# Attention beside an int8 linear layer on one core: the steady state's PSUM, VectorE's small work and SyncE's order rebuilt

## Chip, cores and metric

One core of a Trainium2 chip. The metric is device time in microseconds (us), the median of several runs. TensorE (PE) multiplies, VectorE (DVE), ScalarE (ACT) and GpSimd (POOL) do elementwise work, and SyncE (SP) issues every DMA of this kernel. GpSimd has no operand in PSUM here.

## The reference

For `x` of 8 sequences of 1024 tokens and 256 columns, float32:

```python
xn = layernorm(x)
q = xn @ Wq.T   # 16 heads of 16; k, v: 8 heads of 16, each used by 2 query heads
e = q k^T + alibi_bias              # -|i - j| * 2^-(head + 1)
attn = softmax(e / 4) @ v           # over all 1024 keys, no mask
a = attn @ Wo.T + bo
scale = max(|xn|) / 127             # per token
f = (round(xn / scale) as int8 @ weight_q.T) * scale * weight_scale + bias
out = x + a + f
```

## The kernel before

**Units and tiles.** There are 64 tiles of 128 tokens and 64 units; unit u is one sequence with one key head and its two query heads. A unit computes scores twice. The *row* scores (queries on partitions, `ps_row`) give each query's maximum over all keys; the *column* scores (keys on partitions) are computed with that maximum as two further contraction rows, so that exp can be applied straight away and its result multiplied with the values. q and k are split into three bfloat16 parts (`parts`), written to DRAM, and loaded back per unit as a *row set* (10 DMAs) and a *column set* (10 DMAs and then, for each of two heads, 2 small DMAs of maxima, `place_max`). Alongside, every unit prepares one later tile (11 ahead: normalise, quantise, project to q, k, v, the int8 product) and finishes one earlier tile (9 behind: the output projection).

**Order.** Each engine runs its own written-out order; semaphores join them. `SEGMENTS` cuts the 64 units into stretches with the same set of jobs. In one unit TensorE does 16 steps (s): each computes one 128x1024 block of column scores (`col_block`, two halves of 512) and one block of row scores two units ahead (`row_block`). Every second step it does a value product (`pv_block`, float32). Products whose result has 128 rows are issued as four matmuls of 32 weight columns each (`in_strips`); the tile preparation and projections use whole 128-column weights (L825, L833, L836, L850, L950).

**PSUM.** 8 banks: two row blocks of two banks (`ps_row`), two banks of column scores (`ps_col`), one for values (`ps_pv`), and one, `ps_work`, for everything else. A row block waits until VectorE has reduced the block two before (L635, `reduce_block`). A column half waits until ScalarE's exp (L797) of the same half one step before is done. Seven jobs a unit share `ps_work`, in this order: `turn_max` 0 (L899), `project`, `turn_xn`, `turn_max` 1, `make_qkv`, `turn_xq`, `make_lin`.

**VectorE** reduces 16 row blocks a unit, two after each even step. Between them stand, in this order: `turn_pv` (L660), `find_stats` (L548), `split_max`, `finish` (output sum), `normalise` and `find_scale` (L558 to L571), `quantise`, `find_rest`, `norm` (L667, L674, L681: divides by the softmax sum, gives `att_unit` of the unit before), `split_max`, `scale_lin`.

**GpSimd** multiplies the diagonal blocks of the exp results by the bias on them (L520, `weigh_near`, 8 a unit), and does `find_rstd`, `gather_v`, `find_low` (L481) and `add_linear` (L488, L490).

**SyncE** in one unit: load x, load `att_t` (L359), the column set of unit u+1 (L319, L326), `place_max` 0 (L340), `store_out` (L440), `place_max` 1, the row set of unit u+3, `store_parts` (L297), `store_att` of unit u-1 (L351, two DMAs, waits for `att_unit_ready`). TensorE begins a unit only when all 14 DMAs of its column set have landed:

```python
pe.wait_ge(col_set_loaded[par], 16 * COL_SET * ((u - par) // 2 + 1))
```

## Time and profile before

| | |
|---|---|
| runs | median 1769.76 us of 3 (1768.62 to 1770.13) |
| the profiled execution | 1769.02 us, span 1767.2 us |
| granted TensorE clock, mean | 0.988 |
| TensorE busy | 1707.5 us, 97% |
| VectorE busy | 1594.3 us, 90% |
| ScalarE busy | 1243.0 us, 70% |
| GpSimd busy | 591.9 us, 33% |

A busy TensorE is not TensorE at its peak, as matmuls overlap and their ends are modelled. A "PEld" is a weight load, which runs beside a matmul. "Idle before" names what ended an engine's idle time. DMA issues are SyncE's queue ("SPq"). A row of the timeline has its start and how long it took, in us, and how many instructions it merges.

### The profile page before, as it was taken

What the parts mean: (1) busy time and instruction counts of PE and PEld (TensorE: products, weight loads), DVE (VectorE), ACT (ScalarE), POOL (GpSimd) and SP (SyncE); (2) the same over time, 40 slices, a digit from 0 to 9 for tenths busy, and PEclk for the clock granted to TensorE, in tenths of its full rate; (3) what the DMA queues carried; (4) which work ended last, traced back from release to release, by engine and by line L of the source; (5) the groups of instructions that cost most, each with busy time, mean ns of one, the idle gap of its engine ahead of it and who ended that gap; (6) DMA issues with size and microseconds to landing.
All of it is one profiled execution on the core that took longest, in us unless ns stands there. A gap on an engine that the chain in (4) does not pass through costs nothing.

```text
span 1767.2 us, 68604 instructions
## 1 busy us (share of the span) xinstructions
PE 1707.5 (97%) x22272; PEld 719.4 (41%) x22272; DVE 1594.3 (90%) x2306; ACT 1243.0 (70%) x2498; POOL 591.9 (33%) x904
## 2 busy tenths in 40 slices
PE   6799999999999999999999999999999999999997
PEld 4234443443443443443443443443444444333333
DVE  6899999999999999999999999999999999999991
ACT  3267777777777777777777777777777777777775
POOL 4323333333333333333333333333333333222221
PEclk9799999999999999999999999999999999999999
DMA  4322223223223223223223223223233222222222
GB/s 117 86 71 76 65 70 80 71 79 86 75 78 85 76 78 85 75 79 85 75 79 84 74 81 84 74 81 83 75 81 84 74 81 80 71 72 68 72 63 70
DMA packets 184331, 137.99 MB, mean 78 GB/s; under 512 B 102649, under 2 KB 143865, under 8 KB 184281
## 3 DMA queue, kind: packets, MB, share of 16 engines
q1 hardware_dynamic: 184280, 137.34, 28.8%
q8 instruction: 29, 0.48, 0.1%
q14 instruction: 22, 0.17, 0.0%
HBM read 101.06 MB, written 35.65 MB: 77 GB/s over the span
## 4 chain that ended last, share of the span: by engine, by line
PE 69%; DVE 19%; issue 7%; DMA 1%; DVEq 1%; ACT 1%; SPq 1%; POOL 0%; POOLq 0%; ACTq 0%
PE ps_row L884 20%; PE ps_col L884 19%; PE ps_pv L943 18%; DVE row_max L635 13%; PE ps_work L833 5%; PE ps_work L950 3%; DVE att_normed L674 2%; DVE rest L591 2%; PE ps_work L836 1%; PE ps_work L825 1%; PE ps_work L850 1%; ACT probs L797 1%; DVE rsum L667 1%; DMA bias<-bias_lin 0%; DVEq L231 0%
## 5 line engine op out<-in xcount | busy, mean ns | idle before, releaser
L797 ACT ACTIVATE probs<-ps_col 128x512 f32<-128x512 f32 x2024 | 1098.4, 595 | 293.4 <-PE ps_col L884 293.0
L635 DVE TENSOR_REDUCE row_max<-ps_row 128x1 f32<-128x1024 f32 x1024 | 1201.2, 1213 | 64.4 <-PE ps_row L884 62.8
L520 POOL TENSOR_TENSOR probs<-probs,near 128x256 f32<-128x256 f32 x512 | 376.8, 736 | 1074.0 <-ACT probs L797 1074.0
L884 PE MATMUL ps_col<-q_col,k_col 122*32 122x512 bf16 x8096 | 657.0, 383 | 0.5 <-ACT probs L797 0.4
L884 PE MATMUL ps_row<-k_row,q_row 120*32 120x512 bf16 x8192 | 579.0, 386 | 23.2 <-DVE row_max L635 18.2
L943 PE MATMUL ps_pv<-probs,v_unit 128*32 128x512 f32 x4096 | 530.9, 594 | 3.1 <-POOL probs L520 2.9
L884 PEld LDWEIGHTS ps_col<-q_col,k_col 122*32 122x32 bf16 x8096 | 202.7, 94 | 548.3 <-ACT probs L797 428.6
L884 PEld LDWEIGHTS ps_row<-k_row,q_row 120*32 120x32 bf16 x8192 | 193.5, 95 | 212.7 <-DVE row_max L635 139.6
L943 PEld LDWEIGHTS ps_pv<-probs,v_unit 128*32 128x32 f32 x4096 | 119.6, 110 | 82.4 <-issue 11.9
L833 PE MATMUL ps_work<-xn_t,wqk 128*128 128x128 f32 x636 | 85.1, 284 | 0.0
L833 PEld LDWEIGHTS ps_work<-xn_t,wqk 128*128 128x128 f32 x636 | 75.0, 191 | 22.5 <-issue 22.5
L744 ACT ACTIVATE v_all<-ps_work 128x128 f32 (+1 forms) x53 | 14.7, 277 | 89.8 <-PE ps_work L836 89.8
L660 DVE STREAM_TRANSPOSE pv_turned<-ps_pv 128x512 f32<-128x512 f32 x64 | 45.2, 706 | 20.4 <-PE ps_pv L943 20.4
L950 PE MATMUL ps_work<-wo,att_t 128*128 128x256 f32 x224 | 63.3, 405 | 0.0
L781 ACT ACTIVATE neg_max_t<-ps_work 16x128 bf16<-16x128 bf16 x128 | 34.0, 266 | 37.4 <-PE ps_work L899 34.3
L481 POOL TENSOR_TENSOR parts<-rest,parts 128x384 bf16<-128x384 f32 x64 | 59.1, 923 | 0.9 <-ACT parts L753 0.7
L490 POOL TENSOR_TENSOR base<-base,lin 128x256 f32 (+1 forms) x64 | 46.8, 731 | 11.6 <-POOL base L488 11.2
L488 POOL TENSOR_TENSOR base<-base,bias 128x256 f32 (+1 forms) x64 | 47.1, 736 | 9.7 <-DVE lin L598 8.0
L950 PEld LDWEIGHTS ps_work<-wo,att_t 128*128 128x128 f32 x224 | 37.9, 189 | 27.1 <-issue 24.2
L689 DVE TENSOR_TENSOR out_tile<-ps_work,base 128x256 f32<-128x256 f32 x55 | 23.4, 425 | 20.9 <-issue 15.9
L739 ACT ACTIVATE xn_t<-ps_work 128x256 f32<-128x256 f32 x53 | 20.3, 383 | 29.8 <-PE ps_work L825 29.8
L475 POOL TENSOR_TENSOR rstd<-rstd,half_pow 128x1 f32<-128x1 f32 x64 | 35.8, 559 | 11.9 <-POOL rstd L472 11.0
(74 smaller groups left out, 807.4 us busy)
## 6 DMA issues: line engine op xcount, KB each, us to landing
parts_dram<-parts SPq DMA_DIRECT2D x64, 288.0 KB, 3.2
q_row<-parts_dram SPq DMA_DIRECT2D x128, 96.0 KB
q_col<-parts_dram SPq DMA_DIRECT2D x128, 96.0 KB
q_row<-parts_dram SPq DMA_DIRECT2D x128, 64.0 KB
q_col<-parts_dram SPq DMA_DIRECT2D x128, 64.0 KB
att_dram<-att_unit SPq DMA_DIRECT2D x128, 64.0 KB
att_t<-att_dram SPq DMA_DIRECT2D x56, 128.0 KB, 2.2
out<-out_tile SPq DMA_DIRECT2D x55, 128.0 KB, 1.8
```

The source lines that it names most:

```text
L475: pool.tensor_tensor(rstd[:, par, 1:2], rstd[:, par, 0:1], half_pow[:, :], ALU.pow).then_inc(rstd_ready, 1)
L481: pool.tensor_tensor(parts[:, par, 2, :], rest[:, par, :], parts[:, par, 1, :], ALU.subtract).then_inc(low_ready, 1)
L488: pool.tensor_tensor(here, here, bias[:, :], ALU.add).then_inc(base_ready, 1)
L490: pool.tensor_tensor(here, here, lin[:, par, :], ALU.add).then_inc(base_ready, 1)
L520: pool.tensor_tensor(here, here, near[:, bass.ds(u % KV_HEADS, 1), :].rearrange("p a (e n) -> p (a e) n", e=GROUP), ALU.mult).then_inc(wei ...
L635: dve.tensor_reduce(row_max[:, e, qb:qb + 1], ps_row[qb % 2][:, :], AX_X, ALU.max).then_inc(row_max_found, 1)
L660: dve.transpose(pv_turned[:, :], ps_pv[:, :]).then_inc(pv_read, 1)
L797: act.activation(probs[:, c % PBUFS, e, h * HALF:(h + 1) * HALF], col_bank(f, s, h), ACT.Exp, scale=SCALE).then_inc(exp_done, 1)
L833: pe.matmul(bank[:, m * P:(m + 1) * P], wqk[:, c, m * P:(m + 1) * P], xn_t[:, c, :], start=(c == 0), stop=(c == EC - 1))
L884: mm = pe.matmul(to[at, :], weights[:, at], moving, start=start, stop=stop)
L943: mm = pe.matmul(ps_pv[32 * j:32 * j + 32, :], v_unit[:, par, c, :], probs[:, c % PBUFS, j // 2, (j % 2) * HALF:(j % 2 + 1) * HALF], start ...
L950: mm = pe.matmul(bank, att_of_tile[:, c, :], wo[:, c, :], start=(c == 0), stop=(c == EC - 1))
```

## The change

- **PSUM.** `ps_col` and `ps_work` become a ring of three banks, `ps_ring`. 36 items a unit go through it in a fixed order: the 32 column halves, and after blocks 2, 5, 6 and 7 one item each: `early_max` (the maxima of head 0), `turns` (`xn` and `xq` turned, the maxima of head 1), `qkv`, `outputs` (the int8 product and the output projection). TensorE fills an item's bank when the item three before it has been freed; ScalarE alone reads and frees them.
- **TensorE.** Whole-width products of the steady state are issued in four strips; `turn_xn` becomes a float32 product with the identity. The value product of block c moves from step 2c + 3 to block c + 2's steps.
- **VectorE** keeps the reductions, `find_stats`, `turn_pv`, `normalise`, `find_scale` and `norm`, after blocks 0, 1, 2, 2 and 3. `norm` thus stands after reduction 8 of 16, where it stood after 12.
- **GpSimd** takes `split_max` (the reduction now negates), `quantise`, `split_qk` (all four steps of the splitting of q and k), `weigh_linear` and `finish`.
- **ScalarE** copies q and k unsplit, scales the int8 product per token, copies the projection.
- **SyncE's order** becomes: x (12 ahead, was 11), `att_t`, column set u+1, `store_parts` of the tile before, `place_max` 0, `store_att` of unit u-1, row set u+3, `store_out`, `place_max` 1.

The diff, cut to its core:

```diff
@@ module level and PSUM
+    others = {2: "early_max", 5: "turns", 6: "qkv", 7: "outputs"}
+    for c in range(BLOCKS):
+        items += [(c, e, h) for e in range(GROUP) for h in range(2)]
+        if c in others:
+            items.append(others[c])
-        ps_col = [ctx.enter_context(nc.psum_tensor(f"ps_col{i}", [P, HALF], F32)) for i in range(2)]
+        ps_ring = [ctx.enter_context(nc.psum_tensor(f"ps_ring{i}", [P, HALF], F32))
+                   for i in range(BANKS)]
-        ps_work = ctx.enter_context(nc.psum_tensor("ps_work", [P, HALF], F32))
@@ sync: unit
-                if f["prep"]:
-                    if f["proj"]:
-                        wait_apart(sp, out_ready, u - OUT_BEHIND)
-                    next_x(u + PREP_AHEAD)
+                if f["next_x"]:
+                    next_x(u + X_AHEAD)
                 if f["proj"]:
                     load_att_t(u - OUT_BEHIND, (par + OUT_BEHIND) % 2)
...
-                    wait_apart(sp, col_scores, 2 * SLOTS * u)
+                    wait_apart(sp, ring_filled, ITEMS * u)
                     load_col_set(u + 1, 1 - par)
+                if f["lag"]:
+                    store_parts(u + PREP_AHEAD - 1, (par + PREP_AHEAD - 1) % 2)
+                if not f["last"]:
                     place_max(u + 1, 1 - par, 0)
-                if f["proj"]:
-                    store_out(u - OUT_BEHIND, (par + OUT_BEHIND) % 2)
-                if not_last:
-                    place_max(u + 1, 1 - par, 1)
+                if f["prev"]:
+                    store_att(u - 1)
                 if f["row_set"]:
...
                     load_row_set(u + 3, 1 - par)
-                if f["prep"]:
-                    store_parts(u + PREP_AHEAD, (par + PREP_AHEAD) % 2)
-                if f["prev"]:
-                    store_att(u - 1)
+                if f["out"]:
+                    store_out(u - OUT_BEHIND - 1, (par + OUT_BEHIND + 1) % 2)
+                if not f["last"]:
+                    place_max(u + 1, 1 - par, 1)
@@ gpsimd
+            def split_qk(t, par):
+                wait_apart(pool, ring_freed, ITEMS * (t - PREP_AHEAD) + PLACE["qkv"] + 1)
+                wait_apart(pool, parts_stored[par], 16 * ((t - par) // 2))
+                pool.tensor_copy(parts[:, par, 0, :], qk[:, par, :]).then_inc(high_ready, 1)
...
+                pool.tensor_tensor(rest[:, par, :], qk[:, par, :], parts[:, par, 0, :],
+                                   ALU.subtract).then_inc(rest_ready, 1)
...
+                pool.tensor_copy(parts[:, par, 1, :], rest[:, par, :]).then_inc(middle_ready, 1)
+                find_low(t, par)
...
+                if f["prev"] and not f["last"]:
+                    split_max(GROUP * u + 2, 0)
+                if f["lag"]:
+                    split_qk(t - 1, 1 - tpar)
                 for c in range(BLOCKS):
                     weigh_near(u, c)
+                    if c == 0 and f["prep"]:
+                        find_rstd(t, tpar)
+                    if c == 1 and f["lag"]:
+                        weigh_linear(t - 1, 1 - tpar)
+                        add_linear(t - 1, 1 - tpar)
...
                     if c == 2 and f["prep"]:
+                        quantise(t, tpar)
+                    if c == 3 and f["row_heads"] >= 1:
+                        split_max(GROUP * u + 3, 1)
+                    if c == 3 and f["out"]:
+                        finish(u - OUT_BEHIND - 1, (par + OUT_BEHIND + 1) % 2)
@@ vector: unit
+                for c in range(BLOCKS):
+                    for i in (2 * c, 2 * c + 1):
+                        if i < BLOCKS and f["row_heads"] >= 1:
+                            reduce_block(GROUP * u + 3, 1, i)
+                        if i >= BLOCKS and f["row_heads"] >= 2:
+                            reduce_block(GROUP * u + 4, 0, i - BLOCKS)
+                    if c == 0 and f["prep"]:
...
+                        find_stats(t, tpar)
+                    if c == 1 and f["prev"]:
                         turn_pv(u - 1)
+                    if c == 2 and f["prep"]:
                         normalise(t, tpar)
                         find_scale(t, tpar)
-                    if s == 11 and f["prev"]:
+                    if c == 3 and f["prev"]:
                         norm(u - 1)
@@ tensor
+            def take_bank(u, item):
+                if not (isinstance(u, int) and ITEMS * u + PLACE[item] < BANKS):
+                    pe.wait_ge(ring_freed, ITEMS * u + PLACE[item] - BANKS + 1)
+                return ring_bank(item)
...
+                for c in range(BLOCKS):
+                    if c == 0:
+                        pe.wait_ge(col_set_loaded[par], 16 * COL_SET * ((u - par) // 2 + 1))
+                    col_half(u, par, c, 0, 0)
+                    col_half(u, par, c, 0, 1)
+                    ahead_row_block(u, par, f, 2 * c)
+                    col_half(u, par, c, 1, 0)
+                    if c >= 2:
+                        pv_block(u, par, c - 2)
+                    elif f["prev"]:
+                        pv_block(u - 1, 1 - par, BLOCKS - 2 + c)
+                    col_half(u, par, c, 1, 1)
+                    ahead_row_block(u, par, f, 2 * c + 1)
...
```

## Rows read from the trace of the kernel before

**Rows 1.** The page: busy time of each engine (share of the span), and the chain that ended last

```profile
PE 1707.5 (97%) x22272; PEld 719.4 (41%) x22272; DVE 1594.3 (90%) x2306; ACT 1243.0 (70%) x2498; POOL 591.9 (33%) x904
...
PE 69%; DVE 19%; issue 7%; DMA 1%; DVEq 1%; ACT 1%; SPq 1%; POOL 0%; POOLq 0%; ACTq 0%
...
L739 ACT ACTIVATE xn_t<-ps_work 128x256 f32<-128x256 f32 x53 | 20.3, 383 | 29.8 <-PE ps_work L825 29.8
```

**Rows 2.** The transpose in `turn_pv`, once a unit, in three stretches: ns min/median/max, first and last start

```profile
L660 DVE STREAM_TRANSPOSE pv_turned<-ps_pv x9: 703/704/707, 122.0 to 329.4; 128x512 f32<-128x512 f32 x9
...
L660 DVE STREAM_TRANSPOSE pv_turned<-ps_pv x44: 704/706/707, 356.0 to 1496.9; 128x512 f32<-128x512 f32 x44
...
L660 DVE STREAM_TRANSPOSE pv_turned<-ps_pv x8: 704/705/707, 1520.6 to 1687.9; 128x512 f32<-128x512 f32 x8
```

**Rows 3.** The chain that ended last, in order of time: start us, us, what

```profile
802.24 0.55 PE ps_col L884 x8
802.79 0.86 PE ps_pv L943 x8
...
805.03 0.43 PE ps_col L884 x8
...
813.31 1.06 PE ps_work L950 x4
...
819.89 1.53 PE ps_work L833 x12
```

**Rows 4.** Timeline of VectorE in one unit, with the TensorE row ahead of one reduction

```profile
807.02 0.70 DVE L660 STREAM_TRANSPOSE pv_turned<-ps_pv 128x512 f32<-128x512 f32 x1
...
812.43 0.42 DVE L548 BATCH_NORM_STATS2 stats<-base 128x6 f32 x1
...
813.11 2.35 DVE L635 TENSOR_REDUCE row_max<-ps_row 128x1 f32<-128x1024 f32 x2
...
816.60 0.41 DVE L558 TENSOR_SCALAR xn<-base,mean_var,rstd 128x256 f32 x1
...
817.86 2.35 DVE L635 TENSOR_REDUCE row_max<-ps_row 128x1 f32<-128x1024 f32 x2
...
821.80 0.61 PE L884 MATMUL ps_row<-k_row,q_row 120*32 120x512 bf16 x8
...
822.47 1.22 DVE L635 TENSOR_REDUCE row_max<-ps_row 128x1 f32<-128x1024 f32 x1 [0.21 <-PE ps_row L884]
...
824.08 0.24 DVE L667 RECIPROCAL rsum<-pv_turned 128x16 f32<-128x16 f32 x1
...
825.10 0.45 DVE L681 STREAM_TRANSPOSE att_unit<-att_normed 128x256 f32<-128x256 f32 x1
```

**Rows 5.** Timeline of SyncE's queue (DMA issues) in one unit

```profile
815.86 1.52 SPq L340 DMA_DIRECT2D q_col<-neg_max_t  x2
817.74 0.40 SPq L440 DMA_DIRECT2D out<-out_tile  x1
819.41 1.36 SPq L340 DMA_DIRECT2D q_col<-neg_max_t  x2
821.65 1.74 SPq L319 DMA_DIRECT2D k_row<-parts_dram  x3
...
828.21 0.31 SPq L326 DMA_DIRECT2D k_row<-k_alibi  x1
...
830.01 1.58 SPq L351 DMA_DIRECT2D att_dram<-att_unit  x2
```

**Rows 6.** Timeline where TensorE waits for the first row set

```profile
61.69 0.40 SPq L326 DMA_DIRECT2D k_row<-k_alibi  x1
...
63.60 1.90 PE L884 MATMUL ps_row<-k_row,q_row 120*32 120x512 bf16 x16 [3.69 <-DMA k_row<-k_alibi]
```

**Rows 7.** Timeline of GpSimd in one unit

```profile
801.11 0.92 POOL L481 TENSOR_TENSOR parts<-rest,parts 128x384 bf16<-128x384 f32 x1
...
805.59 0.73 POOL L490 TENSOR_TENSOR base<-base,lin 128x256 f32 x1 [0.19 <-POOL base L488]
```

More of the change, by code:

```diff
@@ L711, in unit @@
                         normalise(t, tpar)
                         find_scale(t, tpar)
-                    if s == 9 and f["prep"]:
-                        quantise(t, tpar)
-                    if s == 11 and f["prep"]:
-                        find_rest(t, tpar, work[1])
-                    if s == 11 and f["prev"]:
+                    if c == 3 and f["prev"]:
                         norm(u - 1)
-                    if s == 14 and f["row_heads"] >= 2:
-                        split_max(GROUP * u + 4, 0)
@@ L721, in unit @@
-                    if s == 15 and f["prep"]:
-                        scale_lin(t, tpar, work[0])
             run_units(dve, unit)
@@ L800, in unit @@
[L800 to L815 removed]
+                keep_first_max(e)
@@ new lines, in unit @@
+            def unit(u, par, f):
+                for item in RING_ITEMS:
+                    if item == "early_max":
+                        if f["last"]:
+                            keep_nothing(u, item)
+                        else:
+                            wait_item(u, item)
+                            keep_max_t(u, par, 0, ring_bank(item))
+                    elif item == "turns":
+                        if f["last"]:
+                            keep_nothing(u, item)
+                        else:
+                            keep_turns(u, par, f)
+                    elif item == "qkv":
+                        if f["prep"]:
+                            keep_qkv_whole(u, par)
+                        else:
+                            keep_nothing(u, item)
+                    elif item == "outputs":
+                        keep_outputs(u, par, f)
+                    else:
+                        exps(u, *item)
@@ L946, in pv_block, with ahead_row_block, turn_nothing @@
                 mm.then_inc(pv_done, 1)
+            def ahead_row_block(u, par, f, i):
+                if i < BLOCKS and f["row_heads"] >= 1:
+                    row_block(GROUP * u + 3, 1 - par, 1, i)
+                if i >= BLOCKS and f["row_heads"] >= 2:
+                    if i == BLOCKS:
+                        wait_row_set(u + 2, par)
+                    row_block(GROUP * u + 4, par, 0, i - BLOCKS)
+            def turn_nothing(u, item):
+                bank = take_bank(u, item)
+                pe.transpose(max_turn(bank), eye_b[:, 0:MAX_ROWS * BLOCKS], eye_b[:, :]).then_inc(
+                    ring_filled, 1)
@@ new lines, in outputs @@
+            def outputs(u, par, f):
+                t, bank = u + PREP_AHEAD, take_bank(u, "outputs")
+                if f["prep"]:
+                    pe.wait_ge(xq_t_ready, t + 1)
+                    for c in range(EC):
+                        mm = in_strips(bank[:, 0:EMBED], xq_t[:, c, :], w8[:, c, :], c == 0,
+                                       c == EC - 1)
+                if f["proj"]:
+                    pe.wait_ge(att_t_loaded, 16 * (u - OUT_BEHIND + 1))
+                    opar = (par + OUT_BEHIND) % 2
+                    for c in range(EC):
+                        mm = in_strips(bank[:, EMBED:2 * EMBED], att_t[:, opar, c, :], wo[:, c, :],
+                                       c == 0, c == EC - 1)
+                else:
+                    mm = pe.transpose(max_turn(bank), eye_b[:, 0:MAX_ROWS * BLOCKS], eye_b[:, :])
+                mm.then_inc(ring_filled, 1)
@@ L948, in project @@
+            run_units(pe, unit)
+            for c in (BLOCKS - 2, BLOCKS - 1):
+                pv_block(UNITS - 1, (UNITS - 1) % 2, c)
             def project(att_of_tile, bank):
```

386 lines of the change are left out of this document (212 added, 174 removed).

## The prediction, made before the run

> **What bounds the kernel now.** I read the page's shares first: TensorE 97% busy, VectorE 90%, ScalarE 70%, GpSimd 33%, and the chain that ended last is 69% TensorE and 19% VectorE [rows 1]. Then the period, from the transpose that runs once a unit [rows 2]: (329.4 - 122.0) / 8 = 25.9 us while no projection runs, (1496.9 - 356.0) / 43 = 26.5 us over the long middle, (1687.9 - 1520.6) / 7 = 23.9 us when no tile is left to prepare. So time is a period times a number of units, and the change has to be costed as a period.
>
> What of the 26.5 us is TensorE streaming? In the chain [rows 3] eight strip matmuls of 512 columns take 0.43 us. At 2.4 GHz one such stream is 0.213 us, so four strips run together. A value product takes 0.86 us. Per unit: 32 blocks (16 column, 16 row) x 0.43 = 13.8; 8 x 0.86 = 6.9; q, k, v: 8 float32 products of 128 columns, each a quarter of the 0.86, 1.7; projection 2 x 0.43 = 0.86; the rest about 0.5. Sum 23.8. The other 2.7 us are waits and changes between whole weights and strips: the column block behind the whole-width product takes 0.55 against 0.43, and the projection 1.06 against 0.86 [rows 3]; that is 0.12 on the way out and perhaps as much or a little more on the way in, so for five such places a unit I estimate 1.0 to 1.3 us. VectorE's busy 1594.3 us are 24.9 us a unit [rows 1], so it is close behind TensorE. These two bound the kernel together; SyncE and GpSimd don't.
>
> **TensorE's part.** Strips remove the changes (-1.0 to -1.3 us). The ring removes the wait for the exp of the step before (the remainder, some 0.6 us). `turn_xn` as a float32 product streams twice as long, +0.2. New streaming: about 24.3 us, if strips of 128 columns run four abreast as those of 512 do. The trace has no such strip. Lower bound: they stream as above. Upper bound: they cost by the matmul, at the nearest row 0.43 / 8 = 54 ns each [rows 3]; 112 small strip matmuls (64 + 16 + 16 + 8 + 8) would take 6.0 us where they stream 3.3, +2.7 us. I take the lower bound, since 54 ns is what the stream itself accounts for, and keep the upper as a rival. The Trainium skill (TensorE: Matmul & The Clock Gate, Back-to-back issue gap) gives about 81 ns a matmul for sustained weight-load and matmul pairs at 128 columns; by it the 112 small matmuls would take 9.1 us, and the sum of TensorE's own chain would be 5.8 us longer. The row's 54 ns is already under that figure, so the rule doesn't fit this strip form, though no run here shows the narrow ones.
>
> **VectorE's part.** It loses `split_max`, `quantise`, `find_rest`, `finish`, `scale_lin`, some 3 us of 24.9, so about 21.7 us are left: it has slack on average. But what stays is bunched after blocks 0 to 3, in front of the first eight reductions. I lay one unit out from its first column matmul (time 0). A row block can be reduced 0.67 us after its first matmul starts (821.80 to 822.47) and a reduction takes 1.17 (2.35 / 2) [rows 4]. Row 0 starts at 0.43, row 1 at 2.17. Reduction 0 runs from 1.10 to 2.27, reduction 1 from 2.84 to 4.0; `find_stats` 0.68 (812.43 to 813.11) to 4.7; two reductions to 7.0; `turn_pv` 0.70 to 7.7; two reductions to 10.1; `normalise` and `find_scale` 1.26 (816.60 to 817.86) to 11.3; two reductions to 13.7; `norm` 1.47 (824.08 to 825.55), so `att_unit` is ready at **15.1** [rows 4].
>
> TensorE feels this. Row 8 waits for reduction 6 (12.5) where it would be due at 10.9, row 10 for reduction 8 (16.2) where it would be due at 13.5. The stall adds up to 2.7 us and isn't given back, since blocks 5 to 7 carry TensorE's extra products. Add about 0.6 us where the ring waits for ScalarE: the item `turns` takes three evictions (0.38 each for the larger two [rows 1]) before the third next half may use its bank. TensorE's own chain: 24.3 + 2.7 + 0.6 = **27.6 us**, already over 26.5. The gains of the first part are real and are spent here.
>
> **SyncE's part, which I expect to end last.** A unit starts only when `place_max` 1 has landed. Before, that was issued at 819.41, ahead of the row set; then came row set, `store_parts`, `store_att`, with nothing waiting soon. After, `store_att` of unit u-1, which waits for the `norm` above, stands ahead of the row set, and `place_max` 1 behind it. Everything behind the waiting `store_att` is late. From `att_unit` ready [rows 5]: wait and address work 0.36 (as 817.38 to 817.74); `store_att` 1.58; three waits and address work 0.88 (820.77 to 821.65); the row set's ten issues, 821.65 to 828.52, 6.87; 0.36 and `store_out` 0.40; about 0.15 to 0.36 and 0.70 until the second small DMA is issued; then 1.91 from the issue of a last DMA to the first matmul that waits for it (61.69 to 63.60) [rows 6]. Sum 13.2 to 13.4. I take 13.2. The period is 15.1 + 13.2 = **28.3 us**, a closed loop: unit start, eight reductions, `norm`, 13 issues, unit start. Its cover before was half a unit of order; now there is none. The other reordered DMAs (x, `att_t`, the column set, `store_parts`, `place_max` 0) are out by about 11 us, before `att_unit` is ready, and hide.
>
> **GpSimd and ScalarE.** GpSimd takes 3 + 3 + 1 + 1 operations of 256 to 384 columns, each at most 0.73 to 0.92 us, with 0.19 us between dependent ones [rows 7], and 4 tiny ones: at most 10 us more on 9.2 (591.9 / 64) [rows 1], so 19 of 28 us. It could hold up `weigh_near` 0 (due at block 2) behind `split_qk`, about 5.3 us against 6.6. I cost it at nothing; without that cover each microsecond it is late is one on TensorE. ScalarE: 19.4 us (1243.0 / 64) plus less than 1.
>
> **The sum.** Units 1 to 8 have no `store_out`: 28.3 - 0.76 = 27.5 against 25.9, 8 x 1.6 = 13 us. 44 units at 28.3 against 26.5: 44 x 1.8 = 78 us. The eight units that load row sets but prepare no tile lack `find_stats` and `normalise`: `att_unit` at 13.5, period 26.7 against 23.9, 8 x 2.8 = 22 us. First unit and the larger first load of x: 2. Together +115 on the profiled execution's own 1769.0: 1884 us; the median of runs is 0.7 above that execution, so **1885 us**.
>
> **Rivals.**
> 1. *TensorE and VectorE set the period, SyncE doesn't.* If issues or landing are 0.7 us or more quicker than summed, the period is 27.6 and less early and late: 44 x 1.1 + 8 x 1.1 (27.0) + nothing late = about +57, 1826 us. For it: the two chains are close. Against: each SyncE term is a row.
> 2. *Strips cost by the matmul.* TensorE's chain is 27.6 + 2.7 = 30.3: 52 x 3.8 + 22 = about +220, 1990 us. For it: 128-column strips are nowhere in the trace.
> 3. *The other side: faster.* The loop over SyncE doesn't close, because row-set issues get shorter when they start without a full ring of column-set descriptors in flight (k_row alone took 1.74 for three [rows 5]), and GpSimd's relief lets TensorE stream. It decides only if 3.8 us go from the SyncE part and the bunching costs TensorE nothing; then 24.3 us a unit: 44 x -2.2, 8 x -2.4, 8 x -1.9 is about -131, 1638 us. It begins to be faster when 1.8 us go from SyncE's part and 1.1 from TensorE's. Against it: the issues look like SyncE's own work, the same pair of small DMAs taking 1.52 right behind the column set and 1.36 two microseconds later [rows 5].
> 4. *The change doesn't remove stalls, it moves them, and ends even*: the period is 26.5 after all, 1770 us.
>
> **Chances.** SyncE's loop, 0.55; rival 1, 0.2; rival 2 or GpSimd late, 0.11; rival 3, 0.1; rival 4, 0.04. Forecast 1885 us. Its own range is 1850 to 1920 (a landing or address gap off by 0.5 us is 26 us over 52 units). The range that leaves 2 in 10 out takes in rival 1 and half of the GpSimd cases: 1805 to 1940. About 0.2% is what a measurement of this kernel can tell from no change. Faster 0.1, same 0.04, slower 0.86.
>
> **What would show it.** In the trace after: a period of 28.3 us between `turn_pv` transposes, 26.7 late; SyncE waiting some 4 us before each `store_att`, and no other long wait; TensorE's wait at each unit's start, put down to the small DMAs of the maxima; VectorE's reductions 0 to 8 back to back, and idle after reduction 11; row-block waits of 2 to 3 us a unit behind reductions 6 and 8; no loss at the changes of weight width. In the late units TensorE would idle over 3 us at a time; should its granted clock fall there, the late period is longer than my 26.7. Wrong if `place_max` 1 is found issued well before the unit's end, if `att_unit` is ready much before 15 us, or if the small strips are far from 3.3 us a unit.

## The result, and the profile after

The changed kernel takes a median of 2021.33 us in 4 runs (2019.78 to 2029.5), against 1769.76 before (4 runs too): a ratio of 1.143 (1.140 to 1.146), 251.6 us slower. The direction was forecast, the size was not: 1885 us with a range up to 1940.

First the page: busy shares, the instruction queue among the DMA queues, and the chain that ended last, by engine and by line. Its answers before are [rows 1].

```profile
PE 1709.5 (85%) x26876; PEld 769.7 (38%) x26876; DVE 1444.4 (72%) x1736; ACT 1275.8 (63%) x2575; POOL 978.6 (49%) x1580
...
q8 instruction: 252, 4.13, 0.9%
...
PE 28%; SPq 25%; issue 20%; DVE 17%; DMA 6%; DVEq 1%; ACT 1%; POOL 0%; ACTq 0%; POOLq 0%
SPq L351 16%; PE ps_pv L1056 10%; PE ps_ring L1003 10%; PE ps_row L1003 8%; DVE row_max L730 8%; DMA q_col<-neg_max_t 5%; SPq L387 4%; SPq L376 2%; DVE att_normed L767 1%; DVE amax L660 1%; DVE xn L653 1%; DVE pv_turned L753 1%; DVE att_unit L774 1%; DVE stats L643 1%; SPq L474 1%
```

TensorE's busy time is what it was (1709.5 against 1707.5 us), but its share of the chain fell from 69% to 28%. SyncE's queue went from 1% to 25%, with nine of the row set's ten issues (L351) as the largest line of all, and "issue" (time in which an engine waited for nothing that the profile shows) from 7% to 20%. The trace of before counts 29 packets of instructions on q8 and this one 252. The prediction had no term for those. Here is the line of before:

```profile
q8 instruction: 29, 0.48, 0.1%
```

Then the period: the `turn_pv` transpose in three stretches, to be read against [rows 2].

```profile
L753 DVE STREAM_TRANSPOSE pv_turned<-ps_pv x9: 704/706/707, 123.7 to 370.9; 128x512 f32<-128x512 f32 x9
...
L753 DVE STREAM_TRANSPOSE pv_turned<-ps_pv x41: 704/706/707, 428.0 to 1664.9; 128x512 f32<-128x512 f32 x41
...
L753 DVE STREAM_TRANSPOSE pv_turned<-ps_pv x7: 705/706/706, 1748.8 to 1915.7; 128x512 f32<-128x512 f32 x7
```

That is 247.2 / 8 = 30.9 us early (forecast 27.5), 1236.9 / 40 = 30.9 in the middle (28.3) and 166.9 / 6 = 27.8 late (26.7). In the middle the units alternate between about 29.4 and 32.3 us, two to a turn of the loop.

Now the loop that was forecast to set the period, in the unit that starts at 1039.77. First VectorE's timeline, then SyncE's queue, then the end of the chain that ended last (start, us, what).

```profile
1040.97 1.22 DVE L730 TENSOR_REDUCE row_max<-ps_row 128x1 f32<-128x1024 f32 x1 [2.65 <-PE ps_row L1003]
...
1046.69 0.71 DVE L753 STREAM_TRANSPOSE pv_turned<-ps_pv 128x512 f32<-128x512 f32 x1
...
1054.68 0.45 DVE L774 STREAM_TRANSPOSE att_unit<-att_normed 128x256 f32<-128x256 f32 x1
```

```profile
1055.58 1.54 SPq L387 DMA_DIRECT2D att_dram<-att_unit  x2
1057.89 2.17 SPq L351 DMA_DIRECT2D k_row<-parts_dram  x3
1060.45 4.62 SPq L351 DMA_DIRECT2D q_row<-parts_dram  x6
1065.25 0.31 SPq L358 DMA_DIRECT2D k_row<-k_alibi  x1
1065.82 0.40 SPq L474 DMA_DIRECT2D out<-out_tile  x1
1066.42 1.50 SPq L376 DMA_DIRECT2D q_col<-neg_max_t  x2
```

```profile
1066.42 0.77 SPq L376
...
1067.24 1.77 DMA q_col<-neg_max_t
1069.01 1.45 issue
1070.46 0.62 PE ps_ring L1003 x5
```

`att_unit` is done at 1055.13, 15.4 us after the unit's start (forecast 15.1); the fifteen issues shown follow with gaps of at most 0.8 us, and the last small DMA lands at 1069.01, 13.9 us later. The next unit could begin there. It begins at 1070.46: 1.45 us go to something on no engine, "issue". SyncE's waits show the same loop over the whole run, as does TensorE's wait at a unit's start (waiter, releaser: us in total, times, longest):

```profile
SPq L274 <- DVE att_unit L774: 214.6, 56, 4.1
```

```profile
PE ps_ring L1003 <- DMA q_col<-neg_max_t: 76.2, 38, 3.3
```

56 waits of 3.8 us before `store_att` (forecast: some 4). Two things beside the loop were not forecast. The first is in TensorE's timeline and in the windows of the same stretch (from:to, us, busy and count of each engine, granted clock, DMA share, GB/s):

```profile
1008.45 0.62 PE L1003 MATMUL ps_ring<-q_col,k_col 122*32 122x512 bf16 x8 [3.01 <-issue]
...
1009.60 1.94 PE L1056 MATMUL ps_pv<-probs,v_unit 128*32 128x512 f32 x8
...
1017.91 1.06 PE L1056 MATMUL ps_pv<-probs,v_unit 128*32 128x512 f32 x8 [1.10 <-DVE pv_turned L753]
...
1026.70 0.62 PE L1003 MATMUL ps_row<-k_row,q_row 120*32 120x512 bf16 x8 [0.66 <-DVE row_max L730]
```

```profile
1008.00:1013.50 5.50, 5.05 (x56) 2.09 (x60) 1.86 (x2) 2.49 (x5) 2.20 (x4) 0.69 0.31 91
1013.50:1031.50 18.00, 15.80 (x246) 6.32 (x238) 16.25 (x22) 12.85 (x27) 11.04 (x18) 1.00 0.22 56
```

TensorE has idled 3.01 us before this unit, the last 1.72 of them after the small DMA had landed (at 1006.73, by the chain). The granted clock of the next 5.5 us is 0.69, so most of them ran at 1.2 GHz; the value product takes 1.94 us against 1.06 eight microseconds on. This unit's `att_unit` is ready 17.1 us after its start, not 15.4. The second: the value product of block 0 waits 1.10 us for `turn_pv`, which reads the same bank of values.

### The profile page after: what moved, and what is told of

Read it like the earlier page. It is cut to its first block, busy times and chain, and to the rows that moved or that the text cites. A ratio compares the mean times of both kernels' runs of the same rounds, so it can differ in the third digit from the quotient of the medians.

```text
span 2017.7 us, 77945 instructions
## 1 busy us (share of the span) xinstructions
PE 1709.5 (85%) x26876; PEld 769.7 (38%) x26876; DVE 1444.4 (72%) x1736; ACT 1275.8 (63%) x2575; POOL 978.6 (49%) x1580
## 4 chain that ended last, share of the span: by engine, by line
PE 28%; SPq 25%; issue 20%; DVE 17%; DMA 6%; DVEq 1%; ACT 1%; POOL 0%; ACTq 0%; POOLq 0%
SPq L351 16%; PE ps_pv L1056 10%; PE ps_ring L1003 10%; PE ps_row L1003 8%; DVE row_max L730 8%; DMA q_col<-neg_max_t 5%; SPq L387 4%; SPq L376 2%; DVE att_normed L767 1%; DVE amax L660 1%; DVE xn L653 1%; DVE pv_turned L753 1%; DVE att_unit L774 1%; DVE stats L643 1%; SPq L474 1%
## 5 line engine op out<-in xcount | busy, mean ns | idle before, releaser
L865 ACT ACTIVATE probs<-ps_ring 128x512 f32<-128x512 f32 x2048 | 1132.1, 595 | 493.4 <-PE ps_ring L1003 461.6
L1003 PE MATMUL ps_ring<-q_col,k_col 122*32 122x512 bf16 x8192 | 754.4, 389 | 135.4 <-DMA q_col<-neg_max_t 76.2
L1003 PE MATMUL ps_row<-k_row,q_row 120*32 120x512 bf16 x8192 | 654.1, 392 | 78.4 <-DVE row_max L730 63.5
L1003 PEld LDWEIGHTS ps_ring<-q_col,k_col 122*32 122x32 bf16 x8192 | 232.2, 97 | 525.4 <-issue 182.6
L1003 PEld LDWEIGHTS ps_row<-k_row,q_row 120*32 120x32 bf16 x8192 | 217.0, 98 | 455.8 <-DVE row_max L730 187.8
L570 POOL TENSOR_SCALAR xclip<-xn,xinv 128x256 f32<-128x256 f32 x53 | 61.1, 1152 | 73.8 <-DVE xinv L666 73.8
L1003 PE MATMUL ps_ring<-xn_t,wqk 128*32 128x128 f32 x2544 | 78.6, 272 | 0.0
L1003 PEld LDWEIGHTS ps_ring<-xn_t,wqk 128*32 128x32 f32 x2544 | 70.4, 109 | 11.1
L573 POOL TENSOR_SCALAR xround<-xclip 128x256 f32<-128x256 f32 x53 | 57.3, 1080 | 9.7 <-POOL xclip L570 9.5
L1003 PE MATMUL ps_ring<-wo,att_t 128*32 128x256 f32 x880 | 56.9, 378 | 0.0
L577 POOL TENSOR_SCALAR xq<-xround 128x256 bf16<-128x256 f32 x53 | 46.1, 871 | 14.5 <-POOL xround L573 14.3
L586 POOL TENSOR_TENSOR rest<-qk,parts 128x384 f32<-128x384 f32 x53 | 48.5, 916 | 9.5 <-POOL parts L584 9.2
```

The source lines that it names most:

```text
L570: pool.tensor_scalar(xclip[:, :], xn[:, par, :], xinv[:, par, :], Q_MAX, ALU.mult, ALU.min).then_inc(xq_ready, 1)
L573: pool.tensor_scalar(xround[:, :], xclip[:, :], -Q_MAX - 1, ROUND, ALU.max, ALU.add).then_inc(xq_ready, 1)
L586: pool.tensor_tensor(rest[:, par, :], qk[:, par, :], parts[:, par, 0, :], ALU.subtract).then_inc(rest_ready, 1)
L865: act.activation(probs[:, c % PBUFS, e, h * HALF:(h + 1) * HALF], ring_bank((c, e, h)), ACT.Exp, scale=SCALE).then_inc(ring_freed, 1)
L1003: mm = pe.matmul(to[at, :], weights[:, at], moving, start=start, stop=stop)
```

## The experiments

"On after" and "on before" say from which kernel each starts. The ratio is to the kernel before, run beside it on the same chip.

### The order of SyncE's queue

**e1_order**, on after: `store_att` last.

```diff
                     place_max(u + 1, 1 - par, 0)
-                if f["prev"]:
-                    store_att(u - 1)
                 if f["row_set"]:
...
                     place_max(u + 1, 1 - par, 1)
+                if f["prev"]:
+                    store_att(u - 1)
```

> The changed kernel with SyncE's order alone altered: row set, store_out, place_max 1, and only then store_att. Theory A (the period is a loop over SyncE: unit start, norm, store_att, row set, place_max 1, unit start; 29.4 us in the undisturbed units, 31.0 us on average): the loop is gone, TensorE's own chain with VectorE is left, about 28 us a unit, and the time falls to 1840 to 1880 us. Theory B (what costs is the reload of TensorE's instructions in each loop turn, with the half clock behind it): the reload stays, the time stays within 20 us of 2020. Theory C (TensorE's and VectorE's bunched work is the period anyway): less than 60 us are gained.

Measured: 1940.99 us, 1.098 (1.094 to 1.101), 80 us faster than after. Its chain has 1% of SyncE's queue where after has 25%:

```profile
PE 53%; DVE 20%; issue 18%; ACT 3%; POOL 2%; DVEq 2%; DMA 1%; SPq 1%; ACTq 1%; POOLq 0%
```

The loop is gone, and the kernel is still 171 us slower than before. Its units in the middle alternate between 28.2 us and 30.5 to 32.6, and it still counts 252 packets on q8. None of the three theories had this size: more than the 60 us of theory C, less than theory A's. The hole at the unit's start is there without SyncE's loop too:

```profile
921.18 0.61 PE L1003 MATMUL ps_ring<-q_col,k_col 122*32 122x512 bf16 x8 [2.95 <-issue]
```

So something besides the loop costs more than the loop does.

**e5_before_order**, on before: the other way round, `store_att` put ahead of the row set and `place_max` 1 behind it, where `norm` stands after reduction 12.

```diff
-                if not_last:
-                    place_max(u + 1, 1 - par, 1)
+                if f["prev"]:
+                    store_att(u - 1)
                 if f["row_set"]:
...
-                if f["prev"]:
-                    store_att(u - 1)
+                if not_last:
+                    place_max(u + 1, 1 - par, 1)
```

> The kernel before with one edit, SyncE's order: store_att ahead of the row set, and place_max 1 last in the unit. Nothing else is changed, and its turn of the loop fits. Theory A (a loop over SyncE): att_unit is ready 22.1 us after the unit's first matmul (803.48 to 825.55), and 13 to 14 us of issues and landing follow, so 35 to 37 us a unit: 2250 to 2400 us. Rival (SyncE's order matters little, since its queue has 10% to spare): 1769 to 1800 us.

Measured: 2429.59 us, 1.373 (1.370 to 1.376), slower than expected; the page's chain has SPq 22%, SPq L319 15% of it. The middle's 41 periods are 37.6 us each:

```profile
L660 DVE STREAM_TRANSPOSE pv_turned<-ps_pv x42: 716/717/718, 422.2 to 1963.0; 128x512 f32<-128x512 f32 x42
```

TensorE waits so long at each unit's start that its mean granted clock is 0.865 in this run, against 0.988 before. With a later `norm` the same order costs 11 us a unit (37.6 against 26.5): the loop is shown from both sides.

### Strips or whole weights

**e2_wide**, on after: the tile's products on whole 128-column weights again (and `xn` turned by a transpose, as before), all else as after.

```diff
-                        in_strips(bank[:, m * P:(m + 1) * P], wqk[:, c, m * P:(m + 1) * P],
-                                  xn_t[:, c, :], c == 0, c == EC - 1)
+                        pe.matmul(bank[:, m * P:(m + 1) * P], wqk[:, c, m * P:(m + 1) * P],
+                                  xn_t[:, c, :], start=(c == 0), stop=(c == EC - 1))
...
```

> The changed kernel with the five products of the tile work on whole 128-column weights again, so that TensorE has some 336 instructions fewer in a turn of the loop. Theory A plus B: the instruction transfers inside the loops vanish as in the kernel before (29 in all, not 252), the granted clock stays at 1.00 in the long stretch, and every second unit no longer takes 3 us more: period 29.4 us in all units, time 1930 to 1950 us. Theory A alone: the period is SyncE's loop and does not move, 2015 to 2025 us. If the changes of weight width were worth more than all that, the time would be above 2021.

Measured: 1922.66 us, 1.087 (1.083 to 1.091), 99 us faster than after. The edit brings back the changes of width, whose removal was forecast as a gain of 1.0 to 1.3 us a unit. Here are the transpose and the q8 packets of the same stretch, first of e2, then the packets of after from 428 to 1665 us:

```profile
L753 DVE STREAM_TRANSPOSE pv_turned<-ps_pv x42: 705/706/707, 435.0 to 1616.7; 128x512 f32<-128x512 f32 x42
```

```profile
q8 instruction: 4, 0.07, 0.0%
```

```profile
q8 instruction: 180, 2.95, 1.0%
```

28.8 us a unit, nearly the same from unit to unit (28.6 to 29.0 us), and 4 packets in the stretch where after has 180 (nine to a turn of the loop, 16 KB each). This is the forecast loop alone: 28.8 where 28.3 was summed. The time is a little under the 1930 to 1950 us that were expected. But the chain of e2 has as large a share of "issue" as that of after:

```profile
SPq 26%; PE 26%; issue 20%; DVE 19%; DMA 6%; DVEq 1%; ACT 1%; POOL 0%; POOLq 0%; ACTq 0%
```

So that share doesn't measure the loading of instructions.

**e3_order_wide**, on after: the diffs of e1 and e2 together.

> Both edits: SyncE's order and whole 128-column weights. Theory A plus B: no loop over SyncE and no reload. What is left is TensorE's chain with VectorE's bunched work, 27.6 us by the forecast's sum plus 1.0 to 1.2 for the width changes, minus what was already counted twice: 27.5 to 28.5 us a unit, 1820 to 1870 us. If the bunching does not cost what the forecast said, the period is 25 to 26.5 us and the time 1690 to 1770 us.

Measured: 1869.46 us, 1.057 (1.054 to 1.060). So the order is worth 53 us where no instructions are loaded (e2 to e3) and 80 where they are (after to e1); strips cost 72 us without the loop (e3 to e1) and 99 with it. The period of e3 is 1050.9 / 37 = 28.4 us (431.4 to 1482.3 us, 38 transposes): the chain of TensorE and VectorE, forecast at 27.6 with strips.

**e4_before_strips**, on before: the five products in strips, order and PSUM as before.

```diff
-                        make_qkv(t, work[1])
+                        strips_qkv(t, work[1])
...
-                        project(att_t[:, (par + OUT_BEHIND) % 2, :, :], work[1][:, 0:EMBED])
+                        strips_project(att_t[:, (par + OUT_BEHIND) % 2, :, :],
+                                       work[1][:, 0:EMBED])
...
-                        turn_xn(t, tpar, work[0])
+                        strips_xn(t, tpar, work[0])
...
```

> The kernel before with the one edit that its five whole-width products of the steady state are issued in strips. Theory B (the longer instruction stream of a loop turn is loaded anew each turn, and TensorE waits for it): some 9 instruction transfers in each turn, 1.5 to 4 us lost in each of 26 turns, half clock after some of them, against at most 1 us a unit gained from the width changes: 1770 to 1850 us. Rival (a reload hides, only the width changes count): 1.0 us a unit faster, about 1710 us. Rival 2 of the prediction (strips cost by the matmul): 2.7 us a unit slower, about 1910 us.

Measured: 1947.81 us, 1.102 (1.098 to 1.105): 178 us slower by this edit alone, far over the 1770 to 1850 us that theory B gave. TensorE's timeline across the end of a loop's turn, the windows around it and the q8 packets from 930 to 960 us:

```profile
939.32 1.03 PE L943 MATMUL ps_pv<-probs,v_unit 128*32 128x512 f32 x8
942.95 0.39 PE L884 MATMUL ps_col<-q_col,k_col 122*32 122x512 bf16 x2 [2.60 <-issue]
946.08 1.04 PE L884 MATMUL ps_col<-q_col,k_col 122*32 122x512 bf16 x6 [2.74 <-issue]
946.49 2.34 PE L884 MATMUL ps_row<-k_row,q_row 120*32 120x512 bf16 x16
```

```profile
918.00:935.00 17.00, 16.99 (x301) 8.07 (x305) 16.21 (x26) 11.87 (x25) 4.83 (x9) 1.00 0.24 71
935.00:952.00 17.00, 11.33 (x147) 4.71 (x137) 9.59 (x12) 7.01 (x15) 4.57 (x7) 0.80 0.33 91
952.00:970.00 18.00, 17.63 (x319) 8.40 (x313) 16.78 (x27) 12.42 (x26) 4.67 (x8) 1.00 0.13 37
```

```profile
q8 instruction: 6, 0.10, 1.3%
```

Nobody is waited for at 939 to 946 us: two column matmuls are issued between two holes of 2.6 and 2.7 us. The packets are spread over the 30 us, and one comes in during each hole (the same view counts one from 939.5 to 942.9 and one from 943.4 to 946.0). That the packets of q8 are TensorE's is inferred: only TensorE's program grew in e4, and q8 goes from 29 packets to 269 over the run while the other instruction queue, q14, stays at 21 (22 before). Then the clock is down (0.80 over the window) and sixteen matmuls take 2.34 us that take 1.04 elsewhere. A unit without this takes 27.0 us, one with it 33.9: about 7 us a turn. The 27.0 is itself over before's 26.5, so the undisturbed unit doesn't gain by the strips either.

**e8_before_unroll4**, on before: `UNROLL = 4` for 2, so that each turn of the loop holds four units. No product changes, and each unit does what it did.

```diff
-UNROLL = 2
+UNROLL = 4
```

> The kernel before, untouched but for UNROLL 4 instead of 2: the same instructions in the same order, a turn of the loop twice as long (about 3046 records of TensorE in four units, not 1523 in two). Theory B (a turn that does not fit TensorE's instruction store is loaded anew and TensorE waits at its start): instruction transfers in every turn, about 7 us lost in each of 13 turns, with the half clock after them: 1840 to 1880 us. Rival (the strips themselves cost what e4_before_strips lost): 1765 to 1772 us.

Measured: 1845.57 us, 1.044 (1.041 to 1.047), as expected. From 360 to 1484 us it has 130 packets on q8 (and 161 on a second instruction queue, q14) where before has 3; the four units of a turn take 26.5, 31 to 32.4, 27.3 and 26.5 us. The strips' streaming is out of the question here: the size of the loop's body brings the packets, and the loss comes with them. The body grows for every engine in e8, so it is e4 that ties the loss to TensorE's.

**Where it begins.** Three more on before put fewer products into strips: **e9_before_qkv_strips** q, k and v alone (the first two lines of e4's diff), **e13_before_small_strips** the others without those, **e14_before_most_strips** all but the int8 product and the turn of `xq`.

> The kernel before with only the q, k, v product in strips: 192 records more in a turn, about 1715 of TensorE. It looks where the store ends. Theory B, store smaller than 1715: transfers in each turn, 6 to 7 us lost per turn, 1930 to 1950 us. Store larger: 29 transfers in all, no loss, and 0.0 to 0.3 us a unit less for one width change, 1755 to 1770 us.

> Where TensorE's instruction store ends: the kernel before with all but q, k, v in strips, 152 records more in a turn, 1675. In e9_before_qkv_strips 1715 fitted in the middle (26.26 us a unit), but units 1 to 8 loaded. If the store holds a number of instructions between 1715 and 1867: no transfers in the middle, 26.0 to 26.4 us a unit there. Units 1 to 8 (no projection, fewer records) show whether it is the number alone: with it, they fit too.

> The kernel before with q, k, v, the projection and the turning of xn in strips: 296 records more in a turn, 1819. Either it fits (26.0 to 26.5 us a unit, about 1765 us) and the store ends between 1819 and 1867, or it loads in each turn as e4_before_strips does (27 and 34 us, about 1945 us) and ends between 1715 and 1819. If the loss grew with the number of instructions over the store and not by the turn, it would be clearly less than the 7 us a turn of e4_before_strips.

Measured: 1769.99 us, 1.0007 (0.9991 to 1.0024); 1911.62 us, 1.081 (1.078 to 1.083); 1874.88 us, 1.060 (1.057 to 1.062). e13 came out against its expectation: it loads in the middle, with fewer records than e9. e14 fell between its two cases: it loads in every turn, but a turn loses about 3 us (units of 27.0 and 30.0), not 7. So the loss doesn't grow evenly with the body. e13 holds both cases in one run. Its transposes and q8 packets, early (122 to 332 us), then in the middle (417 to 1588 us):

```profile
L660 DVE STREAM_TRANSPOSE pv_turned<-ps_pv x9: 698/699/705, 123.1 to 331.7; 128x512 f32<-128x512 f32 x9
```

```profile
q8 instruction: 7, 0.11, 0.2%
```

```profile
L660 DVE STREAM_TRANSPOSE pv_turned<-ps_pv x40: 698/709/718, 417.7 to 1588.3; 128x512 f32<-128x512 f32 x40
```

```profile
q8 instruction: 176, 2.88, 1.0%
```

Early, where the body has no projection, 26.1 us a unit (25.9 before) and hardly a packet; in the middle 30.0 and nine packets a turn. I counted TensorE's records of every kind in one turn of each loop. At 1523 (before), 1527 (e2, e3) and 1609 (e13 early) no instructions are loaded; at 1675 (e13), 1697 (e9 early), 1819 (e14), 1867 (e4), 1870 (after) and 3040 (e8) they are in every turn. But at 1715 (e9, middle) they are not, and in e12 below, at 1719, they are in every second turn. So the size decides only roughly; what decides between 1675 and 1719 wasn't settled. e9 shows what the strips of q, k and v save where nothing is loaded: 26.53 - 26.26 = 0.27 us a unit (its middle against before's), given back in the early units (27.8 us against 25.9).

### What is left: VectorE's bunch and GpSimd

**e10_before_pool**, on before: quantising and `split_max` on GpSimd, nothing else.

```diff
@@ gpsimd: unit
+                    if c == 2 and f["row_heads"] >= 1:
+                        split_max(GROUP * u + 3, 1)
+                    if c == 4 and f["prep"]:
+                        quantise(t, tpar)
...
@@ vector: unit
-                    if s == 9 and f["prep"]:
-                        quantise(t, tpar)
...
```

> The kernel before with one part of the change alone: quantise and split_max go from VectorE to GpSimd (1.7 of VectorE's 24.9 us a unit), order and PSUM as before. If VectorE's load is half of what bounds the kernel: 0.3 to 0.8 us a unit less, 1735 to 1755 us. If TensorE's streaming and width changes bound it: 1765 to 1772 us. If GpSimd's slower operations (1.15, 1.08 and 0.87 us where VectorE takes 0.34, 0.29 and 0.29) come late for turn_xq or hold up the diagonal blocks: above 1772 us.

Measured: 1768.40 us, 0.9993 (0.9983 to 1.0002): no difference, though VectorE's busy time falls from 1594.3 to 1500.0 us. This relief of VectorE alone buys nothing in the old order.

From e3 on, each of four kernels adds one edit to the one before it.

**e6_norm_late**: `norm` after block 6 for 3, out of the bunch.

```diff
-                    if c == 3 and f["prev"]:
+                    if c == 6 and f["prev"]:
                         norm(u - 1)
```

> The kernel of e3_order_wide (28.4 us a unit) with norm moved on VectorE from behind reduction 8 to behind reduction 14, where TensorE's extra products leave VectorE idle. Theory C (the bunched VectorE work stalls TensorE by the row banks, and what is bunched ahead is never given back): 1.0 to 1.4 us a unit less, 27.0 to 27.4 us, 1800 to 1815 us. Rival (TensorE has that stall anyway, from its own extra products and the ring): within 0.3 us a unit of 28.4, above 1850 us.

Measured: 1833.17 us, 1.037 (1.034 to 1.040), 36 us faster than e3, less than expected; the period goes from 28.4 to 27.8.

**e7_proj_early**: the output projection moved from the item after block 7 to the one after block 2, `finish` after block 1, and `turn_pv` directly behind the third reduction, so that the first value product need not wait for it. ScalarE gets one more small copy a unit, which frees the old item.

```diff
                     if c == 2:
...
+                        if f["proj"]:
+                            pe.wait_ge(att_t_loaded, 16 * (u - OUT_BEHIND + 1))
...
+                                mm = pe.matmul(bank[:, 0:EMBED], att_t[:, opar, k, :],
+                                               wo[:, k, :], start=(k == 0), stop=(k == EC - 1))
...
+                        if i == 2 and f["prev"]:
+                            turn_pv(u - 1)
...
-                    if c == 3 and f["out"]:
+                    if c == 1 and f["out"]:
                         finish(u - OUT_BEHIND - 1, (par + OUT_BEHIND + 1) % 2)
```

> As e6_norm_late, and the output projection moved from the item after block 7 into the item of the maxima after block 2, so that TensorE has its own extra work where VectorE is behind; turn_pv stands directly behind reduction 3 of 16, finish after block 1. Theory C: 1.0 to 1.3 us less than e6_norm_late, 25.8 to 26.3 us a unit, 1735 to 1770 us. Rival: no less than e6_norm_late.

Measured: 1807.46 us, 1.022 (1.019 to 1.025), 26 us faster, less than expected. A new wait took the rest (waits view):

```profile
ACT proj L914 <- POOL out_tile L605: 114.3, 43, 2.9
```

ScalarE waits 2.7 us a unit for `finish` on GpSimd to free the buffer of the projection, and the bank of the ring with it.

**e7b_finish_early**: `finish` behind the first diagonal block.

```diff
+                    if c == 0 and f["out"]:
+                        finish(u - OUT_BEHIND - 1, (par + OUT_BEHIND + 1) % 2)
                     if c == 0 and f["prep"]:
...
-                    if c == 1 and f["out"]:
-                        finish(u - OUT_BEHIND - 1, (par + OUT_BEHIND + 1) % 2)
```

> As e7_proj_early, and GpSimd's finish moved from behind the linear sums to directly behind the first diagonal block. In e7_proj_early ScalarE's copy of the projection waited for it, 114 us in 43 units, and with it the ring and TensorE, about 1.4 us a unit. If that wait was the last thing in TensorE's way there: 1.0 to 1.4 us a unit less than 27.4, 26.0 to 26.4 us, 1745 to 1765 us. If another wait takes its place: above 1790 us.

Measured: 1775.91 us, 1.003 (1.001 to 1.005), 32 us faster than e7 and between the two cases that were expected. The wait is gone, and GpSimd is late elsewhere:

```profile
PEld ps_pv L1060 <- POOL probs L555: 53.0, 51, 1.5
```

The value product waits for `weigh_near`, which stands behind the other work of GpSimd.

**e11_pool_order**: quantising after block 3 for 2, the sum of the int8 product after block 5 for 1.

```diff
-                    if c == 1 and f["lag"]:
+                    if c == 5 and f["lag"]:
                         weigh_linear(t - 1, 1 - tpar)
...
-                    if c == 2 and f["prep"]:
+                    if c == 3 and f["prep"]:
                         quantise(t, tpar)
```

> As e7b_finish_early, with GpSimd's order altered: quantise behind the fourth diagonal block instead of the third, the linear sums behind the sixth instead of the second. In e7b_finish_early TensorE waited about 1.5 us a unit for GpSimd at one value product (80 us in all). If that wait was the last thing in its way: 0.8 to 1.3 us a unit less than 26.7, 25.4 to 25.9 us, 1705 to 1740 us, faster than the kernel before. If the row banks or the ring take its place: 1760 to 1775 us.

Measured: **1736.11 us, 0.981 (0.980 to 0.983)**, within the time expected and faster than both kernels. Its middle:

```profile
L753 DVE STREAM_TRANSPOSE pv_turned<-ps_pv x44: 704/705/707, 379.9 to 1490.1; 128x512 f32<-128x512 f32 x44
```

25.8 us a unit against 26.5. It keeps the ring and the work moved to GpSimd and ScalarE, with the places that e6 to e11 gave the work; whole weights and `store_att` last are before's.

**e12_pool_order_strips**: e11 with q, k and v in strips.

```diff
-                        pe.matmul(bank[:, m * P:(m + 1) * P], wqk[:, c, m * P:(m + 1) * P],
-                                  xn_t[:, c, :], start=(c == 0), stop=(c == EC - 1))
+                        in_strips(bank[:, m * P:(m + 1) * P], wqk[:, c, m * P:(m + 1) * P],
+                                  xn_t[:, c, :], c == 0, c == EC - 1)
...
```

> As e11_pool_order, with q, k, v alone in strips (192 records of TensorE more in a turn). If TensorE sets the period there: 0.2 to 0.3 us a unit less in the middle, as e9_before_qkv_strips showed (26.53 to 26.26), 8 to 14 us, minus what is lost if a turn in units 1 to 8 or in the middle does not fit: a loss of 7 us a turn would show as 252 instead of 40 instruction transfers and 1850 us or more.

Measured: 1811.55 us, 1.023 (1.021 to 1.025), 75 us slower than e11, for 96 more matmuls a turn and their weight loads: its units take 25.9 us, and 31 to 32 in every second turn, where q8 has most of its packets. The 8 to 14 us that were expected as a gain are lost in it.

## Why the prediction was right in direction and wrong in size

What the loop over SyncE would do was right. The step that failed is "Strips remove the changes (-1.0 to -1.3 us)" with what follows it, "I take the lower bound": the strips were costed by their streaming alone. What a strip is besides, four instructions for one, had no term, though by the diff the tile's products go from 26 matmuls a unit to 112, and its rivals priced a stream, not a program.

Of the 251.6 us, the trace gives by stretch (after less before, from the first and last transposes): early 8 periods 247.2 - 207.4 = 40 us (forecast 13); then 43 periods from 370.9 to 1696.4 us, 1325.5 - 43 x 26.53 = 185 (forecast 78); the last nine, to 1940.4 us, 26 (forecast 22). The miss of 136 us is in the early and middle units.

- **The missing term.** after to e2 measures it, net of what the strips save: 99 us, of which none was forecast. It is time lost to holes while instructions come in and the lower clock behind them. e8 shows it with no strip added, e4 with no new order.
- **SyncE's loop**: confirmed in place and nearly in size. `att_unit` at 15.4 against 15.1 (the sum is right, though it speaks of 13 issues where there are 15); from there to the landing 13.9 and, in the unit before, 14.1 against 13.2. q_row's six issues and k_row's three took 6.8 us alone, the whole row set 7.7 against 6.87. Sum 29.3; e2 measured 28.8 against 28.3. Over 44 units that is some 22 us of the miss, and early and late units the rest. Early, e2 has 224.8 / 8 = 28.1, 0.7 under its middle, as the 0.76 for the missing `store_out` had it:

```profile
L753 DVE STREAM_TRANSPOSE pv_turned<-ps_pv x9: 704/706/707, 123.5 to 348.3; 128x512 f32<-128x512 f32 x9
```

  Late, the forecast was 1 us short in after: in the unit that starts at 1799.35 `att_unit` is ready at 14.5, where 13.5 was summed, and SyncE's part takes 13.1. The clock, which the prediction feared for there, held: 0.99 granted from 1748 to 1916 us. In e2 seven late transposes lie 28.1 us apart (1672.2 to 1841.0 us), at 0.96; why it is longer there wasn't followed.
- **TensorE's and VectorE's chain**: 27.6 forecast; e3 has 28.4 with whole weights and e1's undisturbed units 28.2 with strips. It was sized 0.6 short. The prediction's own sum shows a gap of that size: 26.5 less at most 1.3 for the changes and 0.6 for the ring, plus 0.2, is 24.8, not 24.3. Rival 1 could not have come true: even without SyncE's loop the kernel is at 1941 us.
- **Width changes** were over-sized. In after the strips of q, k, v take 1001.34 - 999.59 = 1.75 us, from their first start to the next column block's. In e3 the whole products took 1.98 (901.29 to 903.27). That is 0.23 us, and e9 gave 0.27, which is the forecast's price for one place. But the other places don't give it: e13 has three of them (all but the projection) in strips early, with hardly a packet, and takes 26.1 against 25.9, and e3 against e1 shows 0.2 for all five.
- **Rival 2 is refuted.** The same 64 matmuls in 1.75 us are 27 ns each, half of the 54 ns it priced:

```profile
999.59 1.48 PE L1003 MATMUL ps_ring<-xn_t,wqk 128*32 128x128 f32 x48
1000.90 0.61 PE L1003 MATMUL ps_ring<-wv,xn_t 128*32 128x128 f32 x16
1001.34 0.61 PE L1003 MATMUL ps_ring<-q_col,k_col 122*32 122x512 bf16 x8
```

  The narrow strips run four abreast as the wide ones do. The 81 ns a matmul that the Trainium skill gives at 128 columns (TensorE: Matmul & The Clock Gate, Back-to-back issue gap) is three times what this row shows, so it doesn't carry over to column strips.
- **The stall by `norm`'s place** was right in kind: up to 2.7 us were summed for the bunch, and moving `norm` out gave 0.6. The matmuls of after wait 63.5 us in all for reductions, 1.0 a unit; their weight loads wait 187.8 us, but run beside other matmuls, so how much of that is lost isn't shown.
- **GpSimd at nothing** held in after, whose chain has 0% of it, but not once TensorE went faster: in e7b it ends the value product's wait, and e11's gain of 40 us is GpSimd's order alone.
- **The ring** has no run of its own. The wait that it was to remove is smaller: weight loads for column scores waited 428.6 us for an exp before and 159.3 in e11, while the matmuls themselves had waited 0.4 us before. e11, with the ring, the moved work and the new places, but neither strips nor `store_att` ahead of the row set, is 1.9% faster than before; how much of that is the ring's, VectorE's relief or the places' was not separated (e10 shows that two thirds of the relief, without the ring, are worth nothing).

## What to carry to other kernels

When an edit multiplies instructions inside a loop, count each engine's instructions in one turn of it and compare the instruction queue's packets between the traces: here 150 to 350 more a turn took TensorE from none to nine loads in each, and such a turn lost 3 to 7 us (though 192 more in e9's middle brought none). Before a wait is put ahead of other DMAs in one queue, close the loop on paper: what becomes ready when, how many issues stand behind it, and whether the next unit's start is among them. And look for "issue" in the timeline, hole by hole, beside the instruction packets: the share in the chain doesn't tell, as it is 20% in after and 20% in e2, where nothing is loaded and the kernel is 99 us faster.

## What the runs showed of the hardware that was not expected

- **Instruction loading stalls the engine inside a steady loop.** Nine packets of 16 KB a turn, with holes of 2.6 to 3.0 us in the rows shown, with 1675 and from 1819 TensorE records a turn up; none up to 1609; from 1697 to 1719 sometimes.
- **The clock can fall behind such a hole**: after idling 3.0 us TensorE's granted clock was 0.69 over 5.5 us. In e5, with its waits at the units' starts, the mean over the run was 0.865. But not every idle of this length does it: in the late units of after TensorE idles 3.0 to 3.3 us before its starts at 1770.16, 1799.35 and 1826.95, at 0.99 granted over the stretch.
- **GpSimd is slow at these operations with a scalar.** The three quantising steps in after (columns: line, shapes, count, busy, mean ns, idle before):

```profile
L570 POOL TENSOR_SCALAR xclip<-xn,xinv 128x256 f32<-128x256 f32 x53 | 61.1, 1152 | 73.8 <-DVE xinv L666 73.8
...
L573 POOL TENSOR_SCALAR xround<-xclip 128x256 f32<-128x256 f32 x53 | 57.3, 1080 | 9.7 <-POOL xclip L570 9.5
...
L577 POOL TENSOR_SCALAR xq<-xround 128x256 bf16<-128x256 f32 x53 | 46.1, 871 | 14.5 <-POOL xround L573 14.3
```

  1.15 us for a multiplication by a value per token and a minimum, with one full operand, more than the 0.73 of an operation with two [rows 7] that I had taken as the upper bound, and 3.1 times VectorE's mean of 369 ns before. The third step has one operation alone and bfloat16 out, and still takes 0.87. The Trainium skill (GPSIMD Engine Reference, Engine selection) calls one-input work on GpSimd roughly line-rate; the first row speaks against that for float32 with a scalar operand and two operations in one instruction.
